# A decoder layer on one core: the value matmuls of the second attention in tiles of 32 rows and 32 columns

## What is computed

```python
Q = (q @ Wq.T + bq).reshape(bs, sl, H, HD)      # H = 16 heads, HD = 32
K = (k @ Wk.T + bk).reshape(bs, sl, H, HD)      # q: the tokens, k and v: the context
V = (v @ Wv.T + bv).reshape(bs, sl, H, HD)
score = jnp.einsum('bshd,bsgd->bshg', Q, K)
weight = jax.nn.softmax(score, axis=-1)
attn = jnp.einsum('bshg,bsgd->bshd', weight, V).reshape(bs, sl, nf)
x = _layernorm(x + attn @ Wo.T + bo)
```

## Time and profile before

| | us |
|---|---|
| median of 3 runs | 2038.64 (2037.61 to 2040.32) |
| the profiled execution | 2038.83 |
| its span, first to last instruction | 2036.8 |
| PE busy | 1910.0 (94%) |
| DVE busy | 1095.2 (54%) |
| ACT busy | 669.0 (33%) |
| POOL busy | 259.2 (13%) |
| TensorE clock granted, mean | 0.98 |

### The profile page before, as it was taken

How to read it: one execution, slowest core, us unless ns; L and a number is a source line. 1 busy time by engine, 2 the same in 40 slices (tenths; PEclk the granted TensorE clock), 3 DMA queues, 4 the chain that set the end, 5 groups by cost and what they waited for, 6 DMA issues and landing times.

```text
span 2036.8 us, 33248 instructions
## 1 busy us (share of the span) xinstructions
PE 1910.0 (94%) x12912; PEld 1513.5 (74%) x12912; DVE 1095.2 (54%) x1780; ACT 669.0 (33%) x1461; POOL 259.2 (13%) x239
## 2 busy tenths in 40 slices
PE   5999995799996899999999999999999999999997
PEld 5777774678875577777777777777777777777775
DVE  4555554567674445563555463554645554635565
ACT  5556654211220333342232332332322322323321
POOL 2335334223231000000000000000000000000000
PEclk9999998899997899999999999999999999999999
DMA  2011012100000202021020030020210300200011
GB/s 88 22 31 31 21 31 90 32 21 10 21 0 1 88 1 76 23 68 35 13 82 13 7 87 6 13 80 6 64 29 12 81 12 6 87 6 12 7 47 42
DMA packets 38910, 71.50 MB, mean 35 GB/s; under 512 B 7232, under 2 KB 15552, under 8 KB 38080
## 3 DMA queue, kind: packets, MB, share of 16 engines
q1 hardware_dynamic: 38848, 70.63, 11.3%
HBM read 64.85 MB, written 5.77 MB: 35 GB/s over the span
## 4 chain that ended last, share of the span: by engine, by line
PE 64%; issue 1%; DVE 1%; ACT 1%; POOLq 0%; POOL 0%; DVEq 0%
PE pair L1661 11%; PE pair L1663 11%; PE pair L1662 11%; PE y_ps L1661 3%; PE y_ps L1662 3%; PE qa_ps L1661 3%; PE y_ps L1663 3%; PE qa_ps L1662 3%; PE qa_ps L1663 2%; PE pair L1783 2%; PE pair L1784 2%; PE qd_ps L1830 1%; PE pair L1745 1%; PE qd_ps L1831 1%; PE qd_ps L1662 1%
## 5 line engine op out<-in xcount | busy, mean ns | idle before, releaser
L1661 PE MATMUL pair<-XH,GUH 128*128 128x512 f32 (+1 forms) x960 | 375.9, 392 | 0.0
L1663 PE MATMUL pair<-XH,GUL 128*128 128x512 f32 (+1 forms) x960 | 375.6, 391 | 0.0
L1662 PE MATMUL pair<-XL,GUH 128*128 128x512 f32 (+1 forms) x960 | 374.6, 390 | 0.0
L1575 DVE TENSOR_TENSOR h<-pair,sg 128x512 f32<-128x512 f32 (+1 forms) x120 | 82.8, 690 | 426.3 <-ACT sg L1363 426.1
L1363 ACT ACTIVATE sg<-pair 128x512 f32<-128x512 f32 (+1 forms) x120 | 71.7, 597 | 477.2 <-PE pair L1784 382.1
L1663 PEld LDWEIGHTS pair<-XH,GUL 128*128 128x128 f32 (+1 forms) x960 | 171.7, 179 | 47.7
L1662 PEld LDWEIGHTS pair<-XL,GUH 128*128 128x128 f32 (+1 forms) x960 | 171.8, 179 | 47.4
L1661 PEld LDWEIGHTS pair<-XH,GUH 128*128 128x128 f32 (+1 forms) x960 | 171.6, 179 | 47.1
L1265 POOL TENSOR_TENSOR qb_raw<-qb_raw,qb_scale 128x704 f32<-128x704 f32 x8 | 13.7, 1710 | 1066.4 <-DMA qb_scale<-in_gu_scale 1066.4
L1275 ACT ACTIVATE XH<-xe 128x512 fp32r<-128x512 f32 x128 | 78.8, 633 | 179.0 <-DVE xe L1597 179.0
L262 ACT ACTIVATE p<-s_ps,nm 128x128 f32<-128x128 f32 (+1 forms) x256 | 103.8, 428 | 76.5 <-DVE nm L345 76.5
(11 more groups left out here) (295 smaller groups left out, 4042.3 us busy)
## 6 DMA issues: line engine op xcount, KB each, us to landing
gu_raw<-in_gu SPq DMA_DIRECT2D x20, 512.0 KB, 4.2
wrep<-soft_f SPq DMA_DIRECT2D x64, 128.0 KB
dw_raw<-in_dw SPq DMA_DIRECT2D x10, 512.0 KB, 3.9
xT_raw<-in_xT SPq DMA_DIRECT2D x8, 512.0 KB, 3.8
x_raw<-in_x SPq DMA_DIRECT2D x8, 512.0 KB, 3.6
c_raw<-in_cT SPq DMA_DIRECT2D x8, 512.0 KB, 3.8
out<-xtok SPq DMA_DIRECT2D x4, 1024.0 KB, 4.2
gu_raw<-in_gu SPq DMA_DIRECT2D x10, 384.0 KB, 3.1
```

Of the source, the lines that this page charges most:

```text
L1575: nc.vector.tensor_tensor(h[0:M, b, :], pair[b][1][0:M, :], sg[0:M, b, :], ALU.mult).then_inc(h_rdy, 1)
L1661: mm(out, wh, xh, start=first, stop=False)
L1662: mm(out, wh, xl, start=False, stop=False)
L1663: return mm(out, wl, xh, start=False, stop=last)
```

## The change

The zero-filled tile PB (128 x 32 x 4 x 32) is replaced by PT (128 x 32 x 32) with no zeros, and its memset is gone, so that ACT waits for one constant less. `probs_turned` is one transpose of 128 partitions for each half in place of four of 32. `values` takes for each token t and head class j the four groups g apart: weights `VT[rows, t, :]` of 32 rows and 32 columns, 8 columns of probabilities moved, the result in bank g of `so_ps` and the partitions 32j to 32j+31; these are 32 x 4 x 4 = 512 calls in place of 128. `so_ps` holds the results in another order, and `o_high` and `o_low` read it accordingly. Waits and semaphores stay as they are, but for the count of constants.

```diff
--- before.py
+++ after.py
@@ -591,8 +591,7 @@
         c_raw, half = sb("c_raw", [P, KC, S]), sb("xhalf", [P, 2])
         qk_bias, v_bias = sb("qk_bias", [P, 2, NH]), sb("v_bias", [P, D])
         apart_f, apart, identR = sb("apart_f", [P, 8, 2, NH]), sb("apart", [P, 8, 2, NH], F32R), sb("xidentR", [P, P], F32R)
-
-        PB = sb("pb", [P, 32, 4, 2 * NH])
+        PT = sb("pt", [P, 32, 2 * NH])
         l_c, l_b, consts, const_r = sem("l_c"), sem("l_b"), sem("x_consts"), sem("x_const_r")
 
         def first_loads(sp):
@@ -605,8 +604,7 @@
 
             nc.gpsimd.memset(half[:], -0.5).then_inc(consts, 1)
             nc.gpsimd.memset(apart_f[:], 0.0).then_inc(consts, 1)
-            nc.gpsimd.memset(PB[:], 0.0).then_inc(consts, 1)
-            pool.wait_ge(consts, 3)
+            pool.wait_ge(consts, 2)
             for r in range(0, P, 32):
                 for u in range(2):
                     part = apart_f[r:r + 32, :, u, :]
@@ -757,15 +755,15 @@
             def o_high(b, s):
                 act.wait_ge(o_done, b + 1)
                 after(act, wo_done, 2 * (b - 1) + s + 1)
-                copy(OH[:, s].rearrange("p c (g k m) -> p k (c g) m", g=4, k=4),
-                     so_ps[:, :, S + P * s:S + P * s + P].rearrange("p k (x m) -> p k x m", m=8)).then_inc(oh_rdy, 1)
+                copy(OH[:, s].rearrange("p c (g t) -> p g c t", g=4),
+                     so_ps[:, :, S + P * s:S + P * s + P].rearrange("p g (c t) -> p g c t", t=32)).then_inc(oh_rdy, 1)
 
             def features_out(b, i):
                 act.wait_ge(xt_done, 2 * b + i + 1)
                 alone(act, past)
                 copy(x2T[:, :, bass.ds(b * S + i * P, P)], t_ps[:]).then_inc(xt_rdy, 1)
 
-            act.wait_ge(consts, 11)
+            act.wait_ge(consts, 10)
             copy(apart[:], apart_f[:]).then_inc(const_r, 1)
             copy(identR[:], ident[:]).then_inc(const_r, 1)
             context_high(0)
@@ -844,17 +842,14 @@
 
             def probs_turned(b, w):
                 dve.wait_ge(norm_rdy, 2 * b + w + 1)
-                for g in range(4):
-                    rows = slice(32 * g, 32 * g + 32)
-                    done = nc.vector.transpose(PB[rows, 16 * w:16 * w + 16, g, :],
-                                               pr[rows, 2 * w:2 * w + 2].rearrange("p k m h -> p (k m) h"))
-                done.then_inc(pb_rdy, 1)
+                nc.vector.transpose(PT[:, 16 * w:16 * w + 16, :],
+                                    pr[:, 2 * w:2 * w + 2].rearrange("p k m h -> p (k m) h")).then_inc(pb_rdy, 1)
 
             def o_low(b, s):
                 dve.wait_ge(oh_rdy, 2 * (b + 1))
-                sub(OL[:, s].rearrange("p c (g k m) -> p k (c g) m", g=4, k=4),
-                    so_ps[:, :, S + P * s:S + P * s + P].rearrange("p k (x m) -> p k x m", m=8),
-                    OH[:, s].bitcast(F32).rearrange("p c (g k m) -> p k (c g) m", g=4, k=4)).then_inc(ol_rdy, 1)
+                sub(OL[:, s].rearrange("p c (g t) -> p g c t", g=4),
+                    so_ps[:, :, S + P * s:S + P * s + P].rearrange("p g (c t) -> p g c t", t=32),
+                    OH[:, s].bitcast(F32).rearrange("p c (g t) -> p g c t", g=4)).then_inc(ol_rdy, 1)
 
             def residual(b, i, own):
 
@@ -973,13 +968,14 @@
                 after(pe, ol_rdy, 2 * b)
                 pe.wait_ge(pb_rdy, 2 * (b + 1))
                 alone(pe, past)
-                for k in range(4):
-                    for m in range(8):
-                        t = 8 * k + m
-                        for j in range(4):
-                            out = so_ps[32 * j:32 * j + 32, k, S:2 * S].rearrange("p (x m) -> p x m", m=8)[:, :, m]
-                            probs = PB[:, t].rearrange("p g (x j) -> p x g j", j=4)[:, :, :, j]
-                            done = mm(out, VT[:, t, :], probs, start=True, stop=True, skip_group_check=True)
+
+                for t in range(32):
+                    for j in range(4):
+                        for g in range(4):
+                            rows = slice(32 * g, 32 * g + 32)
+                            out = so_ps[32 * j:32 * j + 32, g, S:2 * S].rearrange("p (x t) -> p x t", t=32)[:, :, t]
+                            done = mm(out, VT[rows, t, :], PT[rows, t, :].rearrange("p (x j) -> p x j", j=4)[:, :, j],
+                                      start=True, stop=True, skip_group_check=True)
                 done.then_inc(o_done, 1)
 
             def outputs(b, i, projected):
```

## The result

| | before | after |
|---|---|---|
| median | 2038.78 us | 2243.71 us |
| range, 4 runs each | 2037.61 to 2040.32 | 2242.31 to 2245.80 |
| ratio, 95% interval | | 1.1002 [1.0986, 1.1019] |
| span of the profiled execution | 2036.8 | 2240.6 |

What follows compares the result with a forecast made beforehand. PE was taken to bound the second attention. From 2038.8 us, code breaks +169, scores +7, jumps +5, clock +26 and transposes -13.5 gave +193.5, so 2232 us; range 2145 to 2286, the forecast's own 2209 to 2286.

Steps and rivals of the forecast that it cites:

- Step (b): Value stages: the longer loop code isn't held, so every batch breaks off for code, 26 us a stage, +169 us.
- some 11 a batch: Sign in the second attention's loop: code transfers on PE's queue throughout 470 to 625 us, some 11 a batch.
- a run longer than a block: Sign against the code claim: value matmuls running on past 128 pairs, one block of 256 instructions, without a break.
- rival of the held loop: Second attention: the long loop's code stays held, middle value stages take 16.0 us, kernel 2150 us; chance 0.20.
- Step (a): Value matmuls: issuing, not columns, sets a pair's price, 15.4 ns, so 1024 pairs need 16.0 us a batch.
- Step (c): Scores of batches 2 to 6 get a code break each, +7 us; the loop's five jumps back cost +5 us.
- Step (d): Before the value matmuls: two transposes replace eight, so PE's waits for them go, -13.5 us.
- Step (e): PE's clock falls after broken-off scores and value stages: 12 new spells of 2.2 us, +26 us.
- spell: A stretch of slow PE clock after a broken-off stage, costing 1.4 to 2.7 us, taken as 2.2.
- Step (f): o_high and o_low copies, PB's dropped memset and the data DMAs: no effect on the time.

Runs made afterwards that it cites:

- new_quarter: The changed kernel with batches 1 to 7's value stage as four passes over the code of tokens 0 to 7, other tokens' results left out: 2104.09 us.
- rot_x4: The kernel before with the four value matmuls of a token issued four times in rotation, 128 rows and 32 columns as before: 2243.82 us.
- the part runs: The kernel before with the rotation of four value matmuls issued twice for half or three quarters of the tokens: 2059.82 us and 2107.88 us.
- part_x2_most: The kernel before with the rotation of four value matmuls issued twice for three quarters of the tokens: 2107.88 us.
- rot_x2: The kernel before with the four value matmuls of a token issued twice in rotation: 2131.43 us.
- old_cols8: The kernel before with value matmuls in batches 1 to 7 moving 8 of their 32 columns, the other groups' results left out: 2032.72 us.
- old_split: The kernel before with the wait for the turned probabilities split, each half of the tokens waiting for its own four transposes: 2023.83 us.

## Why the prediction was right

**Step (b), code: right, somewhat too small.** The forecast was 26 us a stage, measured are 217.2 / 8 = 27.2 us, and +178.4 us in all counted as in the prediction (against 38.8), where it had +169. The 3.47 us from block to block that it took from one distance in batch 7 was the most frequent, but a low one: of 50 distances inside the changed kernel's value stages 20 are 3.5 us and 28 are 3.7 to 4.0. What sets these 3.5 to 4.0 us isn't shown. new_quarter, rot_x4 and the part runs each show the cause apart from the tiles: many small matmuls without new code run through, old tiles with much code break off. That the long loop isn't held was taken as likelier without a row for it. The edge lies between 5.9 and 6.4 blocks of pairs, so 10.9 were far outside. By the Trainium skill (Advanced Engine Details and Errata, "ISA Cache"), with 128 KB on TensorE or 8 blocks, the 6.4 and 6.9 blocks of pairs in part_x2_most and rot_x2 would fit, and they weren't held. That doesn't refute the 8 blocks: a pass over either loop transferred 9.25. It refutes counting pairs alone against them. The prediction's sign, "some 11 a batch", is too low for the same reason: the changed kernel has 12.75. Its sign of being wrong, a run longer than a block, shows in the 168 pairs that open each middle stage; with the 88 that close it they read as 40 pairs of a block that was already there and 128 of the next, as every run between has 128. The rival of the held loop is refuted in its condition, not only in its time.

**Step (a), the price of a pair: wrong, and harmless.** The step reads "a price that the clock doesn't move is one of issuing instructions, not of columns", and took 15.4 ns. Measured are 8.3 ns in the first run of a stage, (1.58 - 0.2) / 167, and 9.2 in the later ones at a clock of 0.50; old_cols8 shows that columns moved are the reason. What misled it was a pair with 32 columns at 15.1 ns at half the clock and 15.0 at full: true, but nothing that rules the columns out. Why the clock doesn't move that pair, no run shows. The error cost nothing because the block's distance, not the pairs in it, set the stage: cheaper pairs made longer breaks, 2.1 to 2.6 us where 1.4 were forecast. The same error made the rival of the held loop too dear by 6 us a batch: it priced 16.0 us where new_quarter has 10.1. All small matmuls in the trace moved 32 columns, so it couldn't tell. What the Trainium skill says (TensorEngine Tiling (Array Packing), "Instruction Overhead") holds in kind, that few columns don't make a matmul cheap in proportion: four times fewer columns made a pair 1.8 times cheaper, not four times. Its equal price for all matmuls under 60 columns doesn't hold: 8 and 32 columns differ.

**Step (c), scores and jumps: sum right, parts wrong.** +12 us were forecast as 7 and 5; the scores alone took +11.9, of which 9.3 are breaks (14 instead of 4) and 2.6 longer runs. At the jumps back PE shows no idle time: no matmul of the mask (L951), the first after a jump, has a wait before it.

**Step (d), transposes: right.** All waits for them are gone, and old_split, which removes all but 1.1 us of the same wait and nothing else, gains 13.5 us (2037.28 to 2023.83), 11.5 of them in waits.

**Step (e), the clock: right in sum, by luck in part.** Forecast +26, measured +25.3. The prediction tied the slow clock to stages that break off. But rot_x4 has as many breaks and loses 10.2 us, and new_quarter has none in its middle stages and loses 8.5; so the breaks alone don't set the 2.2 us of a spell, and what does stays open. (Of the prediction's bounds for a spell, its rows give 1.4 and 2.3 us; the 2.7 has no row.) It was priced as spells after a stage; the trace shows the clock at 0.50 through most of a stage too, which costs little there, as code is what is waited for:

```profile
589.80:615.00 25.20, 9.06 (x856) 8.47 (x855) 0.00 (x0) 0.00 (x0) 0.00 (x0) 0.50 0.08 25
616.00:622.00 6.00, 6.00 (x18) 4.64 (x18) 2.67 (x4) 0.29 (x1) 0.58 (x1) 0.61 0.00 0
```

The first stretch is batch 3's stage, the second what follows: 18 long matmuls in the time that 26 take at full clock.

**Step (f): right.** ACT's copies take 0.593 us each as before (0.595).

## What to carry to other kernels

Count the instructions of a loop body before splitting a matmul into smaller ones: on PE a body of 750 load-matmul pairs was held and one of 814 was transferred anew in every pass, and from then on 128 small pairs cost 3.5 to 4.0 us however cheap each is. Ask also what the split buys: here columns full of zeros were moved at 0.3 ns each, and removing them saved less than the added pairs cost, even with all code in place. And look first at the wait itself: a semaphore wait split in two took away what three fewer transposes a half were to take away.

## What the runs showed of the hardware

- The edge of a held loop is sharp: with pairs for 5.9 blocks of 256 instructions a pass transfers nothing on PE's queue, with pairs for 6.4 it transfers 9.25 blocks, with 6.9 again 9.25, with 10.9 12.75 (mean of four passes each).
- Pairs of f32 matmul and load with 32-column weights take 8.4 ns with 8 columns moved and 15.3 with 32, at 128 rows, if the four tiles of columns alternate; with one tile four times in a row and 32 columns it is 29.8 ns.
- At half the clock the small pairs slow by a tenth (8.3 to 9.2 ns), the matmuls of 512 columns by a factor of 1.8 (0.234 to 0.427 us from start to start).
- The clock also fell in a stage without breaks: new_quarter's, 1024 pairs of 32 rows and 8 columns in 10 us, with 0.88 granted from 470 to 620 us; rot_x4, with breaks but 128 rows and 32 columns, lost 10.2 us to the clock and the changed kernel 25.3. What lowers the clock in these stages isn't shown.
